# An LSTM step with its gate sums in one scale: reductions for scans, tanh's scale from a register

## The chip, the cores and the metric

One core of one Trainium2 chip. The metric is the device time of one execution in microseconds (us), the median of a few runs. Engines: PE (TensorE), DVE (VectorE), ACT (ScalarE), POOL (GpSimd), SP (SyncE, which starts the DMAs).

## The reference

For x of (2, 1024, 256), an LSTM over 1024 steps with hidden size 256 and batch 2, then a mixture of experts over its 2048 tokens, each added to x:

```
a = xW[t] + h @ Wh                      # xW = x @ Wx + b, (2, 1024) per step
i, f, o = sigmoid(a[:, :256]), sigmoid(a[:, 256:512]), sigmoid(a[:, 512:768])
g = tanh(a[:, 768:])
c = f * c + i * g
h = o * tanh(c)
...
x = x + hs                              # all h
x = x + mixture(x)                      # 2 shared experts, 8 routed ones, top 2, gates by sigmoid
```

## The kernel before

Everything lies in SBUF before it is needed; the 1024 steps are 16 tiles of 64. In each step PE, DVE and ACT do the LSTM (`lstm(s)` on each engine), and behind it each engine takes a slice of the mixture of the tile before (`mixture(s, ...)`, with all slots written out by hand by step number). Tile 0 has `first_tile(s)` in their place; after tile 15 the mixture runs once more without the LSTM. In each of the tiles 1 to 15, PE also makes half of the xW part for the tile after the next one, from fp16 parts of x and Wx (L753): six products after step 0 and six after step 4, and then one after each of the steps 5 to 16.

The product h @ Wh is made of fp16 parts: Wh scaled by a power of two as `wh_hi` + `wh_lo`/4096, h in `hh[..., 0]` (low part) and `hh[..., 1]` (high part, about 4096 h). Each gate column has three neighbouring PSUM columns: one in which `wh_lo` x high part stands (L665), one with `wh_hi` x high part (L672, two columns at once with the low part), and one with the step's xW value (`gif_xw`, `o_xw`), written by DVE from `seeds`, which POOL stages in pieces of 8 steps (`stage`). 8 chunks of 128 gate rows, 4 for g and i (`gi`), 2 for f, 2 for o.

One step of the LSTM, with the lines of the profile:

1. PE: low products of f and gi (L665, 12), high products of f (L672, 4) and gi (8), then low and high of o. `s_mul` counts f, gi, o.
2. DVE: `summed` (L562) forms each gate's sum by a scan, state = factor x state + data, over its three columns; the factors `part_fac` are 0, 1/4096 and the inverse of twice the weight scale. f, then gi, then o.
3. ACT: tanh of the third column: `tf` (L325), g and i into `gi_out` (L328), `to` (L332). sigmoid is made from tanh.
4. DVE: (tanh f + 1) x c (L573), the c scan (L579), seeds of the next step (L585), `to1` = 4096 (to + 1) (L587).
5. ACT: `tc` = tanh of c (L335).
6. DVE: `hh` high part = (to + 1) x tc (L590), `h` = to1 x tc in f32 (L595), `c_now` (L597), o's seed (L601), `hh` low part (L603).

The first weight load of the next step on PE waits for L590 (`s_hhi`), the first high product for L603 (`s_hlo`). DVE works in order; it waits on its own results through `s_own`, which L587 and L595 raise, and on ACT through `s_tanh`.

Of the kernel before, what the change touches and what calls it, by code (L numbers as in the profile page):

```python
# [8 lines left out]
ALU = mybir.AluOpType  # L9
ACT = mybir.ActivationFunctionType  # L10
F32 = mybir.dt.float32
F16 = mybir.dt.float16
U32 = mybir.dt.uint32
AX = mybir.AxisListType
RMAX = bass.bass_isa.ReduceOp.max

P = 128
B, T, D = 2, 1024, 256
KC = D // P
H4 = 4 * D  # L20
MC = H4 // P
HC = KC * B
GATES = MC * B
GI, FG, OG = 4 * B, 2 * B, 2 * B
PARTS = 3
LO = 2.0 ** 12
NTOK = B * T
BANK = 512
TS = 64
TT = TS * B  # L30
NT = T // TS
HS = 8
# [47 lines left out]
def cond_resid_kernel(nc, xT, condT, wx, wh, bT, wr, rb, sw1, sw3, sw2, rw1, rw2, eye, iota, outT):  # L80
    with ExitStack() as ctx:
        def sb(name, shape, dt=F32):
            return ctx.enter_context(nc.sbuf_tensor(name, shape, dt))
# [7 lines left out]
        gates = bank("gates", 3)  # L91
        state, up_sh, up_rt, acc_lg, xw_next = (bank(n) for n in ("state", "up_sh", "up_rt", "acc_lg", "xw_next"))

        gi_ps = gates[:, BANK - PARTS * GI:BANK]
        f_ps = gates[:, BANK:BANK + PARTS * FG]
        o_ps = gates[:, 2 * BANK:2 * BANK + PARTS * OG]
        gif_xw = gates[:, BANK - PARTS * GI:BANK + PARTS * FG].rearrange("p (c j) -> p c j", j=PARTS)[:, :, 2]
        o_xw = o_ps.rearrange("p (c j) -> p c j", j=PARTS)[:, :, 2]

        gi_sum = gates[:, 0:PARTS * GI]  # L100
        f_sum = gates[:, 2 * BANK - PARTS * FG:2 * BANK]
        o_sum = gates[:, 3 * BANK - PARTS * OG:3 * BANK]
        cs = state[:, 0:HC * 3].rearrange("p (c j) -> p c j", j=3)
# [10 lines left out]
        xw = sb("xw", [P, (T + TS) * GATES])  # L114
# [25 lines left out]
        scale = sb("scale", [P, 4, 3])  # L140
        tops, s_wh, s_wx, s_xin = scale[:, 0, :], scale[:, 3, 0:1], scale[:, 3, 1:2], scale[:, 3, 2:3]

        sc = sb("sc", [P, 6])
        unit, one_unit, half_lo, s_wh_lo, wh_g, wh_g_lo = (sc[:, j:j + 1] for j in range(6))
        xw_scale = sb("xw_scale", [P, 2])

        largest = sb("largest", [P, MAX_OF])
        first_banks = (up_sh, up_rt, xw_next, state)
        wh_times_lo = xw[:, TS * GATES:TS * GATES + KC * H4].rearrange("p (k n) -> p k n", k=KC)
        hw0 = sb("hw0", [P, GATES])  # L150
        hh = sb("hh", [P, KC, B, 2], F16)
        h32 = sb("h32", [P, 2, HS, HC])
        seeds = sb("seeds", [P, 2, HS, GATES])

        part_fac = sb("part_fac", [P, GI, PARTS])

# [87 lines left out]
        def _(pool):  # L244
# [10 lines left out]
            def stage(q, first):  # L255

                g.tensor_copy(seeds[:, q % 2, :, :].rearrange("p s g -> p (s g)"), xw[:, first]).then_inc(s_staged, 1)

# [53 lines left out]
        def _(act):  # L312
            activation = nc.scalar.activation
            nc.scalar.preload_act_table(ACT.Gelu)

            act.wait_ge(s_scale, 4)
            for dst, dst_lo, src, by, by_lo in ((wh_hi[:, :, 0:D], wh_times_lo[:, :, 0:D], wh_sb[:, :, 0:D], wh_g, wh_g_lo),
                                                (wh_hi[:, :, D:H4], wh_times_lo[:, :, D:H4], wh_sb[:, :, D:H4], s_wh, s_wh_lo)):
                activation(dst, src, ACT.Identity, scale=by)
                activation(dst_lo, src, ACT.Identity, scale=by_lo).then_inc(s_hi, 1)  # L320

            def lstm(s):

                act.wait_ge(s_sum, 4 * s + F_OF)
                activation(tf[:], f_sum.rearrange("p (c j) -> p c j", j=PARTS)[:, :, PARTS - 1], ACT.Tanh, scale=0.5).then_inc(s_tanh, 1)  # L325

                act.wait_ge(s_sum, 4 * s + GI_OF)
                activation(gi_out, gi_sum.rearrange("p (g c j) -> p g c j", g=2, j=PARTS)[:, :, :, PARTS - 1], ACT.Tanh,  # L328
                           scale=0.5).then_inc(s_scan, 1)

                act.wait_ge(s_sum, 4 * s + O_OF)
                activation(to[:], o_sum.rearrange("p (c j) -> p c j", j=PARTS)[:, :, PARTS - 1], ACT.Tanh, scale=0.5).then_inc(s_tanh, 1)  # L332

                act.wait_ge(s_sum, 4 * s + C_OF)
                activation(tc[:], cs[:, :, 2], ACT.Tanh, scale=0.5).then_inc(s_tanh, 1)  # L335
# [51 lines left out]
        def _(dve):  # L387
# [3 lines left out]
            def link(ins):  # L391

                done[0] += 1
                ins.then_inc(s_link, 1)
                dve.wait_ge(s_link, done[0])
# [10 lines left out]

            link(v.memset(part_fac[:], 1.0))
            link(v.memset(part_fac[:, :, 0], 0.0))
            link(v.memset(part_fac[:, :, 1], 1.0 / LO))
            link(v.memset(fac_add[:], 1.0))  # L410
# [15 lines left out]

            for dst, src, by in ((unit, s_wh, 2.0), (s_wh_lo, s_wh, LO), (wh_g, s_wh, 2.0)):
                v.tensor_scalar(dst, src, by, None, ALU.mult).then_inc(s_scale, 1)
            v.tensor_scalar(wh_g_lo, s_wh, 2.0 * LO, None, ALU.mult).then_inc(s_scale, 1)
            dve.wait_ge(s_scale, 4)  # L430
            link(v.reciprocal(one_unit, unit))
            link(v.tensor_copy(part_fac[:, :, 2], one_unit.broadcast_to([P, GI])))
            dve.wait_ge(s_xw0, 48)
# [9 lines left out]

            for j, (lo, hi, chunks) in enumerate(((0, D, range(0, 4)), (D, H4, range(4, MC)))):
                for m in chunks:
                    first_xw(m)
                dve.wait_ge(s_hi, j + 1)
                v.scalar_tensor_tensor(wh_lo[:, :, lo:hi], wh_hi[:, :, lo:hi], -LO, wh_times_lo[:, :, lo:hi],
                                       ALU.mult, ALU.add).then_inc(s_lo, 1)
            dve.wait_ge(s_xwc0, MC)  # L450
# [4 lines left out]
            dve.wait_ge(s_xwc0, MC + 1)  # L455
            v.tensor_copy(gif_xw, xw[:, 0:GI + FG])

            v.tensor_copy(o_xw, xw[:, GI + FG:GATES]).then_inc(s_hhi, 1)
            v.memset(hw0[:], 0.0).then_inc(s_hlo, 1)
# [99 lines left out]

            def summed(dst, ps, n):  # L560

                return v.tensor_tensor_scan(dst, part_fac[:, 0:n, :].rearrange("p c j -> p (c j)"), ps, 0.0, ALU.mult, ALU.add)  # L562

            def lstm(s):
                piece, at = s // HS, s % HS

                dve.wait_ge(s_mul, 3 * s + F_OF)
                summed(f_sum, f_ps, FG).then_inc(s_sum, 1)
                dve.wait_ge(s_mul, 3 * s + GI_OF)
                summed(gi_sum, gi_ps, GI).then_inc(s_sum, 1)  # L570

                dve.wait_ge(s_tanh, 3 * s + TF_OF)
                v.scalar_tensor_tensor(addend[:, :, 2], tf[:], 1.0, c_now[:], ALU.add, ALU.mult).then_inc(s_scan, 1)  # L573
                dve.wait_ge(s_mul, 3 * s + O_OF)
                summed(o_sum, o_ps, OG).then_inc(s_sum, 1)

# [4 lines left out]
                if at == 0:  # L581
# [7 lines left out]
                dve.wait_ge(s_tanh, 3 * s + TC_OF)  # L589
                v.scalar_tensor_tensor(hh[:, :, :, 1], to[:].rearrange("p (k b) -> p k b", b=B), 1.0,  # L590
                                       tc[:].rearrange("p (k b) -> p k b", b=B), ALU.add, ALU.mult).then_inc(s_hhi, 1)

                h_now = h32[:, piece % 2, at, :]
                dve.wait_ge(s_own, 2 * s + 1)
                v.tensor_tensor(h_now, to1[:], tc[:], ALU.mult).then_inc(s_own, 1)  # L595

                ins = v.tensor_scalar(c_now[:], cs[:, :, 2], 0.5, None, ALU.mult)  # L597
                if at in (STAGE_AT, HS - 1):
# [3 lines left out]
                dve.wait_ge(s_own, 2 * s + 2)  # L602
                v.scalar_tensor_tensor(hh[:, :, :, 0], hh[:, :, :, 1], -LO, h_now.rearrange("p (k b) -> p k b", b=B),  # L603
                                       ALU.mult, ALU.add).then_inc(s_hlo, 1)

# [264 lines left out]
```

## Time and profile before

| | |
|---|---|
| Median of 3 runs | 2158.12 us (2157.96 to 2159.33) |
| Span of the profiled execution | 2157.6 us, 94124 instructions |
| PE | 2037.5 us busy, 94% |
| DVE | 1725.5 us busy, 80%, 13239 instructions |
| ACT | 861.0 us busy, 40% |
| POOL | 136.5 us busy, 6% |
| The three scans of L562, 3072 in all | 591.9 us |

Busy times are of one profiled execution, from its first instruction to its last. Its time without the profiler isn't known apart; the span stands 0.5 us below the median of the runs. The granted clock of PE is 0.5 of full speed from about 24 us to the end of the last LSTM step. Matmuls overlap, so that PE's busy share says little of the room left on it.

### The profile page before, as it was taken

To read this page: it belongs to the slowest core of one execution; us is meant where nothing else is said; L and a number is where in the kernel's file an instruction comes from. 1 tells how busy PE (TensorE), PEld (TensorE's weight loads), DVE (VectorE), ACT (ScalarE), POOL (GpSimd) and SP (SyncE) were. 2 spreads that over 40 slices of the span, in tenths; PEclk is the share of its full clock that TensorE was granted. 3 is DMA by queue.
4 is the path that set the end of the run, shared out by engine and by line. 5 is a ranking of instruction groups with operands and counts; after the bars stand their busy time and mean duration, and the time that the engine had idled before them with its cause. 6 is when DMAs were issued, how large, how long until landed. Compare 5 with 4: busy or idle time off the path is not lost. (4 is left out here: it accounts for less than half of the span.)

```text
span 2157.6 us, 94124 instructions
## 1 busy us (share of the span) xinstructions
PE 2037.5 (94%) x37356; PEld 1862.5 (86%) x37356; DVE 1725.5 (80%) x13239; ACT 861.0 (40%) x4505; POOL 136.5 (6%) x457
## 2 busy tenths in 40 slices
PE   8999989899898989989899898998989999898998
PEld 7889979798897979989799797998979889797998
DVE  7888878788787878878788787887878788787884
ACT  4554334344343434434343333443334344343442
POOL 0000000000000000000000000000000000000000
PEclk7555555555555555555555555555555555555557
DMA  5000000000000000000000000000000000000000
GB/s 218 3 3 3 3 5 3 6 3 2 6 3 6 3 5 3 3 6 3 6 3 3 6 3 6 3 3 6 3 6 3 5 3 2 6 3 6 3 3 6
DMA packets 7218, 20.02 MB, mean 9 GB/s; under 512 B 1136, under 2 KB 5616, under 8 KB 5872
## 3 DMA queue, kind: packets, MB, share of 16 engines
q1 hardware_dynamic: 6768, 13.73, 1.7%
q8 instruction: 318, 5.21, 1.0%
q14 instruction: 132, 1.08, 0.2%
HBM read 11.63 MB, written 2.10 MB: 6 GB/s over the span
## 5 line engine op out<-in xcount | busy, mean ns | idle before, releaser
L562 DVE TENSOR_TENSOR_SCAN gates<-part_fac,gates 128x12 f32<-128x12 f32 (+1 forms) x3072 | 591.9, 193 | 373.8 <-PE gates L672 326.1
L665 PE MATMUL gates<-hh,wh_lo 128*128 128x2 f16 x16384 | 749.4, 168 | 103.7 <-issue 90.9
L665 PEld LDWEIGHTS gates<-hh,wh_lo 128*128 128x128 f16 x16384 | 604.8, 105 | 275.5 <-DVE hh L590 154.4
L672 PE MATMUL gates<-hh,wh_hi 128*128 128x4 f16 x16384 | 690.7, 167 | 3.6 <-DVE hh L603 3.6
L672 PEld LDWEIGHTS gates<-hh,wh_hi 128*128 128x128 f16 x16384 | 595.2, 104 | 5.0 <-DVE hh L603 5.0
L325 ACT ACTIVATE tf<-gates 128x4 f32<-128x4 f32 x1024 | 178.1, 174 | 910.8 <-DVE gates L562 908.5
L679 PE MATMUL up_rt<-xt,rw_sb 128*128 128x128 f32 x1024 | 297.1, 445 | 0.6 <-DVE hid_rt L529 0.5
L685 PE MATMUL acc_lg<-hid_rt,rw_sb 128*128 128x128 f32 x1024 | 296.8, 445 | 0.0
L679 PEld LDWEIGHTS up_rt<-xt,rw_sb 128*128 128x128 f32 x1024 | 230.9, 314 | 1.4 <-DVE hid_rt L529 1.4
L685 PEld LDWEIGHTS acc_lg<-hid_rt,rw_sb 128*128 128x128 f32 x1024 | 230.9, 314 | 0.2 <-DVE hid_rt L529 0.2
L332 ACT ACTIVATE to<-gates 128x4 f32<-128x4 f32 x1024 | 177.7, 174 | 121.4 <-DVE gates L562 42.3
L328 ACT ACTIVATE fac_add<-gates 128x8 f32<-128x8 f32 x1024 | 185.4, 181 | 64.9
L579 DVE TENSOR_TENSOR_SCAN state<-fac_add 128x12 f32<-128x12 f32 x1024 | 195.9, 191 | 0.0
L335 ACT ACTIVATE tc<-state 128x4 f32<-128x4 f32 x1024 | 177.7, 174 | 2.6
L587 DVE TENSOR_SCALAR to<-to 128x4 f32<-128x4 f32 x1024 | 174.6, 170 | 4.2
L573 DVE SCALAR_TENSOR_TENSOR fac_add<-tf,c_now 128x4 f32<-128x4 f32 x1024 | 173.1, 169 | 3.8
L590 DVE SCALAR_TENSOR_TENSOR hh<-to,tc 128x4 f16<-128x4 f32 x1024 | 170.3, 166 | 5.7
L603 DVE SCALAR_TENSOR_TENSOR hh<-hh,h 128x4 f16<-128x4 f16 x1024 | 165.9, 162 | 0.0
L595 DVE TENSOR_TENSOR h<-to,tc 128x4 f32<-128x4 f32 x1024 | 159.5, 156 | 0.0
L597 DVE TENSOR_SCALAR c_now<-state 128x4 f32<-128x4 f32 x1024 | 158.9, 155 | 0.0
L601 DVE COPY gates<-seeds 128x4 f32<-128x4 f32 x1024 | 158.6, 155 | 0.0
L585 DVE COPY gates<-seeds 128x12 f32<-128x12 f32 x1024 | 158.0, 154 | 0.0
(129 smaller groups left out, 1814.6 us busy)
## 6 DMA issues: line engine op xcount, KB each, us to landing
rw_sb<-rw SPq DMA_DIRECT2D x2, 2048.0 KB, 23.1
sw_sb<-sw SPq DMA_DIRECT2D x3, 1024.0 KB, 13.1
outT<-osb SPq DMA_DIRECT2D x16, 128.0 KB, 3.9
x_sb<-xT SPq DMA_DIRECT2D x1, 1920.0 KB, 9.4
wh_sb<-wh SPq DMA_DIRECT2D x1, 1024.0 KB, 4.7
wx_sb<-wx SPq DMA_DIRECT2D x1, 1024.0 KB, 6.9
x_sb<-xT SPq DMA_DIRECT2D x1, 128.0 KB, 5.2
eye_sb<-eye SPq DMA_DIRECT2D x1, 64.0 KB, 5.4
```

The source lines that it names most:

```text
L325: activation(tf[:], f_sum.rearrange("p (c j) -> p c j", j=PARTS)[:, :, PARTS - 1], ACT.Tanh, scale=0.5).then_inc(s_tanh, 1)
L328: activation(gi_out, gi_sum.rearrange("p (g c j) -> p g c j", g=2, j=PARTS)[:, :, :, PARTS - 1], ACT.Tanh, scale=0.5).then_inc(s_scan, 1)
L332: activation(to[:], o_sum.rearrange("p (c j) -> p c j", j=PARTS)[:, :, PARTS - 1], ACT.Tanh, scale=0.5).then_inc(s_tanh, 1)
L335: activation(tc[:], cs[:, :, 2], ACT.Tanh, scale=0.5).then_inc(s_tanh, 1)
L562: return v.tensor_tensor_scan(dst, part_fac[:, 0:n, :].rearrange("p c j -> p (c j)"), ps, 0.0, ALU.mult, ALU.add)
L573: v.scalar_tensor_tensor(addend[:, :, 2], tf[:], 1.0, c_now[:], ALU.add, ALU.mult).then_inc(s_scan, 1)
L579: v.tensor_tensor_scan(cs.rearrange("p c j -> p (c j)"), fac.rearrange("p c j -> p (c j)"), addend.rearrange("p c j -> p (c j)"), 0.0, ALU ...
L587: v.tensor_scalar(to1[:], to[:], 1.0, LO, ALU.add, ALU.mult).then_inc(s_own, 1)
L665: mm(columns(ps, j)[:, :, 0], wh_lo[:, c, (m0 + j) * P:(m0 + j + 1) * P], hh[:, c, :, 1], start=(j == 0 and c == 0), stop=False, skip_grou ...
L672: last = mm(columns(ps, j)[:, :, 0:2], wh_hi[:, c, (m0 + j) * P:(m0 + j + 1) * P], hh[:, c, :, :], start=False, stop=True, skip_group_chec ...
L679: last = mm(ps, w[:, c, at:at + P], xt[:, c, :], start=(c == 0), stop=(c == KC - 1))
L685: ins = mm(acc[:, k * TT:(k + 1) * TT], w[:, k * P:(k + 1) * P], hid, start=(first and k == 0), stop=last, skip_group_check=True)
```

## The change

The xW columns are multiplied by 2 x 4096 x the weight scale (`sums_by`) when they are staged by POOL (for the first step, by DVE), `hh`'s low part is no longer divided by anything, and so all three columns of a gate have one scale. In detail:

- `summed` becomes a reduction over the three columns (`tensor_reduce`, add), with 4 or 8 outputs side by side. `part_fac` goes.
- The three tanh activations of the gates read those, and take their scale (0.5 before) from an ACT register `by_sums`, loaded once in the setup from `to_tanh`. The `tc` activation keeps its 0.5.
- `hh`'s high part is now to1 x tc, with DVE's wait for to1 (`s_own`) in front of it, which stood ahead of L595 before. `hh`'s low part is a subtraction.
- POOL's staging is a multiplication with a broadcast scale in place of a copy.
- In the setup ACT makes only `wh_hi`; `wh_lo` is made by DVE from `wh_sb` straight. Some one-column scales go and others come.

```diff
--- before.py
+++ after.py
@@ -97,9 +97,9 @@
         gif_xw = gates[:, BANK - PARTS * GI:BANK + PARTS * FG].rearrange("p (c j) -> p c j", j=PARTS)[:, :, 2]
         o_xw = o_ps.rearrange("p (c j) -> p c j", j=PARTS)[:, :, 2]
 
-        gi_sum = gates[:, 0:PARTS * GI]
-        f_sum = gates[:, 2 * BANK - PARTS * FG:2 * BANK]
-        o_sum = gates[:, 3 * BANK - PARTS * OG:3 * BANK]
+        gi_sum = gates[:, 0:GI]
+        f_sum = gates[:, 2 * BANK - FG:2 * BANK]
+        o_sum = gates[:, 3 * BANK - OG:3 * BANK]
         cs = state[:, 0:HC * 3].rearrange("p (c j) -> p c j", j=3)
 
         xw_first = [xw_next[:, 0:TT], up_rt[:, 0:TT]]
@@ -140,19 +140,16 @@
         scale = sb("scale", [P, 4, 3])
         tops, s_wh, s_wx, s_xin = scale[:, 0, :], scale[:, 3, 0:1], scale[:, 3, 1:2], scale[:, 3, 2:3]
 
-        sc = sb("sc", [P, 6])
-        unit, one_unit, half_lo, s_wh_lo, wh_g, wh_g_lo = (sc[:, j:j + 1] for j in range(6))
+        sc = sb("sc", [P, 5])
+        sums_by, twice_by, to_tanh, half_lo, wh_g = (sc[:, j:j + 1] for j in range(5))
         xw_scale = sb("xw_scale", [P, 2])
 
         largest = sb("largest", [P, MAX_OF])
         first_banks = (up_sh, up_rt, xw_next, state)
-        wh_times_lo = xw[:, TS * GATES:TS * GATES + KC * H4].rearrange("p (k n) -> p k n", k=KC)
         hw0 = sb("hw0", [P, GATES])
         hh = sb("hh", [P, KC, B, 2], F16)
         h32 = sb("h32", [P, 2, HS, HC])
         seeds = sb("seeds", [P, 2, HS, GATES])
-
-        part_fac = sb("part_fac", [P, GI, PARTS])
 
         fac_add = sb("fac_add", [P, 2, HC, 3])
         fac, addend = fac_add[:, 0, :, :], fac_add[:, 1, :, :]
@@ -254,7 +251,8 @@
 
             def stage(q, first):
 
-                g.tensor_copy(seeds[:, q % 2, :, :].rearrange("p s g -> p (s g)"), xw[:, first]).then_inc(s_staged, 1)
+                g.tensor_tensor(seeds[:, q % 2, :, :].rearrange("p s g -> p (s g)"), xw[:, first],
+                                sums_by.broadcast_to([P, HS * GATES]), ALU.mult).then_inc(s_staged, 1)
 
             stage(0, slice(GATES, (HS + 1) * GATES))
 
@@ -313,23 +311,24 @@
             activation = nc.scalar.activation
             nc.scalar.preload_act_table(ACT.Gelu)
 
-            act.wait_ge(s_scale, 4)
-            for dst, dst_lo, src, by, by_lo in ((wh_hi[:, :, 0:D], wh_times_lo[:, :, 0:D], wh_sb[:, :, 0:D], wh_g, wh_g_lo),
-                                                (wh_hi[:, :, D:H4], wh_times_lo[:, :, D:H4], wh_sb[:, :, D:H4], s_wh, s_wh_lo)):
-                activation(dst, src, ACT.Identity, scale=by)
-                activation(dst_lo, src, ACT.Identity, scale=by_lo).then_inc(s_hi, 1)
+            act.wait_ge(s_scale, 2)
+            for dst, src, by in ((wh_hi[:, :, 0:D], wh_sb[:, :, 0:D], wh_g), (wh_hi[:, :, D:H4], wh_sb[:, :, D:H4], s_wh)):
+                activation(dst, src, ACT.Identity, scale=by).then_inc(s_hi, 1)
+
+            act.wait_ge(s_scale, 3)
+            by_sums = nc.scalar.alloc_register("by_sums")
+            nc.scalar.reg_load(by_sums, to_tanh[0:1, :].bitcast(U32))
 
             def lstm(s):
 
                 act.wait_ge(s_sum, 4 * s + F_OF)
-                activation(tf[:], f_sum.rearrange("p (c j) -> p c j", j=PARTS)[:, :, PARTS - 1], ACT.Tanh, scale=0.5).then_inc(s_tanh, 1)
+                activation(tf[:], f_sum, ACT.Tanh, scale=by_sums).then_inc(s_tanh, 1)
 
                 act.wait_ge(s_sum, 4 * s + GI_OF)
-                activation(gi_out, gi_sum.rearrange("p (g c j) -> p g c j", g=2, j=PARTS)[:, :, :, PARTS - 1], ACT.Tanh,
-                           scale=0.5).then_inc(s_scan, 1)
+                activation(gi_out, gi_sum.rearrange("p (g c) -> p g c", g=2), ACT.Tanh, scale=by_sums).then_inc(s_scan, 1)
 
                 act.wait_ge(s_sum, 4 * s + O_OF)
-                activation(to[:], o_sum.rearrange("p (c j) -> p c j", j=PARTS)[:, :, PARTS - 1], ACT.Tanh, scale=0.5).then_inc(s_tanh, 1)
+                activation(to[:], o_sum, ACT.Tanh, scale=by_sums).then_inc(s_tanh, 1)
 
                 act.wait_ge(s_sum, 4 * s + C_OF)
                 activation(tc[:], cs[:, :, 2], ACT.Tanh, scale=0.5).then_inc(s_tanh, 1)
@@ -404,9 +403,6 @@
                 link(v.tensor_scalar(scale[:, 3, at], scale[:, 2, at], 2.0 ** 13, None, ALU.mult))
 
 
-            link(v.memset(part_fac[:], 1.0))
-            link(v.memset(part_fac[:, :, 0], 0.0))
-            link(v.memset(part_fac[:, :, 1], 1.0 / LO))
             link(v.memset(fac_add[:], 1.0))
             link(v.memset(fac[:, :, 0], 0.0))
             link(v.memset(c_now[:], 0.0))
@@ -424,12 +420,11 @@
             dve.wait_ge(s_top, 1)
             power(slice(0, 1))
 
-            for dst, src, by in ((unit, s_wh, 2.0), (s_wh_lo, s_wh, LO), (wh_g, s_wh, 2.0)):
-                v.tensor_scalar(dst, src, by, None, ALU.mult).then_inc(s_scale, 1)
-            v.tensor_scalar(wh_g_lo, s_wh, 2.0 * LO, None, ALU.mult).then_inc(s_scale, 1)
-            dve.wait_ge(s_scale, 4)
-            link(v.reciprocal(one_unit, unit))
-            link(v.tensor_copy(part_fac[:, :, 2], one_unit.broadcast_to([P, GI])))
+            for dst, by in ((wh_g, 2.0), (twice_by, 4.0 * LO)):
+                v.tensor_scalar(dst, s_wh, by, None, ALU.mult).then_inc(s_scale, 1)
+            link(v.tensor_scalar(sums_by, s_wh, 2.0 * LO, None, ALU.mult))
+            dve.wait_ge(s_scale, 2)
+            v.reciprocal(to_tanh, twice_by).then_inc(s_scale, 1)
             dve.wait_ge(s_xw0, 48)
             link(v.tensor_scalar(b_twice[:], b_sb[:, 0:KC], 2.0, None, ALU.mult))
 
@@ -441,21 +436,21 @@
                                 b_sb[:, m:m + 1], 2.0 if m < KC else 1.0, ALU.add, ALU.mult).then_inc(s_xwc0, 1)
 
 
-            for j, (lo, hi, chunks) in enumerate(((0, D, range(0, 4)), (D, H4, range(4, MC)))):
+            for j, (lo, hi, by, chunks) in enumerate(((0, D, wh_g, range(0, 4)), (D, H4, s_wh, range(4, MC)))):
                 for m in chunks:
                     first_xw(m)
                 dve.wait_ge(s_hi, j + 1)
-                v.scalar_tensor_tensor(wh_lo[:, :, lo:hi], wh_hi[:, :, lo:hi], -LO, wh_times_lo[:, :, lo:hi],
-                                       ALU.mult, ALU.add).then_inc(s_lo, 1)
+                v.scalar_tensor_tensor(wh_lo[:, :, lo:hi], wh_sb[:, :, lo:hi], by, wh_hi[:, :, lo:hi],
+                                       ALU.mult, ALU.subtract).then_inc(s_lo, 1)
             dve.wait_ge(s_xwc0, MC)
             v.tensor_tensor(xw[:, 0:GATES], xw[:, 0:GATES], hw0[:], ALU.add).then_inc(s_xwc0, 1)
 
             take_back(dve, s_lg, 1)
             link(v.tensor_copy(tpart[:], logits))
             dve.wait_ge(s_xwc0, MC + 1)
-            v.tensor_copy(gif_xw, xw[:, 0:GI + FG])
-
-            v.tensor_copy(o_xw, xw[:, GI + FG:GATES]).then_inc(s_hhi, 1)
+            v.tensor_scalar(gif_xw, xw[:, 0:GI + FG], sums_by, None, ALU.mult)
+
+            v.tensor_scalar(o_xw, xw[:, GI + FG:GATES], sums_by, None, ALU.mult).then_inc(s_hhi, 1)
             v.memset(hw0[:], 0.0).then_inc(s_hlo, 1)
 
             lg, nl, e, num, dn, sg, mask, t0, t1, t2 = (rt[:, j, :] for j in range(10))
@@ -557,22 +552,22 @@
                     take_back(dve, s_free, 1)
                     v.tensor_tensor(osb[:], acc.rearrange("p (k t) -> p k t", k=KC), xt[:], ALU.add).then_inc(s_fin, 1)
 
-            def summed(dst, ps, n):
-
-                return v.tensor_tensor_scan(dst, part_fac[:, 0:n, :].rearrange("p c j -> p (c j)"), ps, 0.0, ALU.mult, ALU.add)
+            def summed(dst, ps):
+
+                return v.tensor_reduce(dst, ps.rearrange("p (c j) -> p c j", j=PARTS), AX.X, ALU.add)
 
             def lstm(s):
                 piece, at = s // HS, s % HS
 
                 dve.wait_ge(s_mul, 3 * s + F_OF)
-                summed(f_sum, f_ps, FG).then_inc(s_sum, 1)
+                summed(f_sum, f_ps).then_inc(s_sum, 1)
                 dve.wait_ge(s_mul, 3 * s + GI_OF)
-                summed(gi_sum, gi_ps, GI).then_inc(s_sum, 1)
+                summed(gi_sum, gi_ps).then_inc(s_sum, 1)
 
                 dve.wait_ge(s_tanh, 3 * s + TF_OF)
                 v.scalar_tensor_tensor(addend[:, :, 2], tf[:], 1.0, c_now[:], ALU.add, ALU.mult).then_inc(s_scan, 1)
                 dve.wait_ge(s_mul, 3 * s + O_OF)
-                summed(o_sum, o_ps, OG).then_inc(s_sum, 1)
+                summed(o_sum, o_ps).then_inc(s_sum, 1)
 
                 dve.wait_ge(s_scan, 2 * s + 2)
 
@@ -587,11 +582,11 @@
                 v.tensor_scalar(to1[:], to[:], 1.0, LO, ALU.add, ALU.mult).then_inc(s_own, 1)
 
                 dve.wait_ge(s_tanh, 3 * s + TC_OF)
-                v.scalar_tensor_tensor(hh[:, :, :, 1], to[:].rearrange("p (k b) -> p k b", b=B), 1.0,
-                                       tc[:].rearrange("p (k b) -> p k b", b=B), ALU.add, ALU.mult).then_inc(s_hhi, 1)
+                dve.wait_ge(s_own, 2 * s + 1)
+                v.tensor_tensor(hh[:, :, :, 1], to1[:].rearrange("p (k b) -> p k b", b=B),
+                                tc[:].rearrange("p (k b) -> p k b", b=B), ALU.mult).then_inc(s_hhi, 1)
 
                 h_now = h32[:, piece % 2, at, :]
-                dve.wait_ge(s_own, 2 * s + 1)
                 v.tensor_tensor(h_now, to1[:], tc[:], ALU.mult).then_inc(s_own, 1)
 
                 ins = v.tensor_scalar(c_now[:], cs[:, :, 2], 0.5, None, ALU.mult)
@@ -600,8 +595,8 @@
 
                 v.tensor_copy(o_xw, seeds[:, piece % 2, at, GI + FG:GATES])
                 dve.wait_ge(s_own, 2 * s + 2)
-                v.scalar_tensor_tensor(hh[:, :, :, 0], hh[:, :, :, 1], -LO, h_now.rearrange("p (k b) -> p k b", b=B),
-                                       ALU.mult, ALU.add).then_inc(s_hlo, 1)
+                v.tensor_tensor(hh[:, :, :, 0], h_now.rearrange("p (k b) -> p k b", b=B), hh[:, :, :, 1],
+                                ALU.subtract).then_inc(s_hlo, 1)
 
             def round_end():
                 take_back(dve, s_mul, 3 * TS)
```

## Rows read from the trace of the kernel before

**Rows 1.** Waits: engine, tile and line waited for; us in total, times, longest us

```profile
PEld gates L665 <- DVE hh L590: 154.4, 829, 1.7
PEld gates L665 <- issue: 93.2, 28, 4.4
```

**Rows 2.** Timeline of one step: start us, us, engine, line, work, idle before

```profile
1001.70 0.42 DVE L562 TENSOR_TENSOR_SCAN gates<-part_fac,gates 128x12 f32<-128x12 f32 x2 [0.40 <-PE gates L672]
...
1001.92 0.17 ACT L325 ACTIVATE tf<-gates 128x4 f32<-128x4 f32 x1 [1.10 <-DVE gates L562]
...
1002.13 0.17 DVE L573 SCALAR_TENSOR_TENSOR fac_add<-tf,c_now 128x4 f32<-128x4 f32 x1
1002.16 0.18 ACT L328 ACTIVATE fac_add<-gates 128x8 f32<-128x8 f32 x1
1002.21 0.18 DVE L562 TENSOR_TENSOR_SCAN gates<-part_fac,gates 128x12 f32<-128x12 f32 x1
1002.37 0.19 DVE L579 TENSOR_TENSOR_SCAN state<-fac_add 128x12 f32<-128x12 f32 x1
1002.42 0.17 ACT L332 ACTIVATE to<-gates 128x4 f32<-128x4 f32 x1
...
1002.60 0.17 ACT L335 ACTIVATE tc<-state 128x4 f32<-128x4 f32 x1
1002.63 0.17 DVE L587 TENSOR_SCALAR to<-to 128x4 f32<-128x4 f32 x1
1002.80 0.17 DVE L590 SCALAR_TENSOR_TENSOR hh<-to,tc 128x4 f16<-128x4 f32 x1
...
1003.02 0.40 PEld L665 LDWEIGHTS gates<-hh,wh_lo 128*128 128x128 f16 x12 [0.17 <-DVE hh L590]
```

**Rows 3.** DVE groups by shape: count, busy us, mean ns, idle before

```profile
L562 DVE TENSOR_TENSOR_SCAN gates<-part_fac,gates 128x12 f32<-128x12 f32 x2048 | 375.5, 183 | 347.7 <-PE gates L672 326.1
L562 DVE TENSOR_TENSOR_SCAN gates<-part_fac,gates 128x24 f32<-128x24 f32 x1024 | 217.5, 212 | 26.1
...
L595 DVE TENSOR_TENSOR h<-to,tc 128x4 f32<-128x4 f32 x1024 | 159.5, 156 | 0.0
...
L619 DVE TENSOR_REDUCE largest<-x_sb 128x1 f32<-128x256 f32 x16 | 6.6, 411 | 0.0
...
L475 DVE TENSOR_TENSOR rt<-acc_lg,tpart 128x8 f32<-128x8 f32 x16 | 2.7, 167 | 2.4 <-DVEq L220 2.4
...
L547 DVE TENSOR_REDUCE den<-rt 128x1 f32<-128x8 f32 x16 | 2.4, 153 | 0.0
```

**Rows 4.** Line L522: engine, instruction, count, ns min, median, max, first and last start

```profile
L522 DVEq EVENT_SEMAPHORE  x128: 21/21/21, 159.5 to 2134.4; - x128
```

**Rows 5.** Timeline of DVE in the tail of the span: start us, us, engine, line, work

```profile
2130.47 0.15 DVE L547 TENSOR_REDUCE den<-rt 128x1 f32<-128x8 f32 x1
2130.66 0.15 DVE L504 TENSOR_SCALAR den<-den 128x1 f32<-128x1 f32 x1
...
2132.67 0.29 DVE L517 SCALAR_TENSOR_TENSOR uu<-th,up_sh 128x128 f32<-128x128 f32 x1 [0.39 <-ACT th L359]
2133.06 0.29 DVE L524 SCALAR_TENSOR_TENSOR hid_sh<-uu,up_rt 128x128 f32<-128x128 f32 x1
```

**Rows 6.** Lines L342 and L363 on ACT; ns min, median, max

```profile
L363 ACT ACTIVATE xw<-xw_next,b_sb,xw_scale x60: 458/458/463, 151.3 to 2026.8; 128x128 f32 x60
L342 ACT ACTIVATE xw<-xw_next,b_sb x17: 368/368/373, 27.4 to 146.8; 128x128 f32<-128x128 f32 x17
```

**Rows 7.** Timeline of PE, two of the steps that follow a step with one wx product

```profile
167.19 0.51 PE L665 MATMUL gates<-hh,wh_lo 128*128 128x2 f16 x12
...
169.19 0.51 PE L665 MATMUL gates<-hh,wh_lo 128*128 128x2 f16 x12
```

**Rows 8.** Timeline of POOL, one staging copy

```profile
1001.33 0.29 POOL L257 COPY seeds<-xw 128x128 f32 x1 [13.09 <-DVE c_now L597]
```

**Rows 9.** Group of the costliest POOL multiply

```profile
L263 POOL TENSOR_TENSOR x_scaled<-x_sb,scale 128x256 f32<-128x256 f32 x16 | 9.8, 614 | 0.0
```

## The prediction

> **What bounds the kernel now.** I read the totals first, then the list of waits, then the timeline of one step, and last the groups by shape for durations. PE is busy 94% of the span, but the waits say that it is not the bound: in 829 of the 1024 steps the first weight load of a step (L665) stands idle until DVE has written hh at L590 [rows 1]. In another 180 steps (12 in each of 15 tiles, the ones in which one fp16 product for the next tile's wx part stands last on PE) the load is let in at the same moment, but the array is still streaming. In the 15 first steps of a tile PE is late by itself, part of the 28 waits put down to "issue" [rows 1]. So the time is 1024 turns of one loop of dependent work, some 1.95 us each, and what counts is the distance round it.
>
> In the timeline of a step [rows 2] count from the f scan at 1001.70. The f scan and its hand-over bring ACT to tf at +0.22; tf and a hand-over bring DVE to L573 at +0.43; the o scan follows at +0.51; ACT takes `to` at +0.72; L587 (to1) runs from +0.93 to +1.10. This is the **output branch**. The **cell branch** starts with the gi scan at +0.21, goes through L328 (+0.46), the c scan L579 (+0.67) and `tc` (+0.90), and ends at +1.07. L590 starts at +1.10, 0.03 after the end of `tc`, and this is where the reader should look: to1 ends at the very moment at which L590 starts. Today L590 doesn't read to1. After the change it does. Each hand-over from one engine to another costs 0.03 to 0.04 us.
>
> **The sums.** The three scans become reductions with as many columns in and a third as many out. A scan of 12 columns takes 183 ns and one of 24 takes 212 [rows 3]. No multi-output reduction is in the trace; the nearest are 8 columns to one in 153 ns and 256 to one in 411, a slope of 258/248 = 1.04 ns a column [rows 3]. That gives 157 ns for 12 columns and 170 for 24. They read PSUM; an addition of 8 columns with one PSUM operand takes 167 against 156 for 4 columns from SBUF [rows 3], of which 4 are columns, so I add 8: **165 and 178**. The f and o reductions then take 18 ns less each, gi 34 less. Below, the bound is no PSUM surcharge (26 less each); above, a reduction that pays for each of its outputs and so costs what the scan does (0 less). I take 18, since the rows it rests on are of the same instruction.
>
> The output branch holds two of these terms (f, o): to1 ends 0.036 earlier, at +1.064. The cell branch holds only gi, since the gi scan is let in by PE and not by the f scan's end: `tc` ends 0.034 earlier, at +1.036.
>
> The Trainium skill ("VectorE: DVE Perf Modes", Rules for kernel authors) calls `tensor_reduce` the slowest DVE operation on a hot path and advises against it. The rows have it at 153 ns where the 12-column scan takes 183 [rows 3]; by the page nothing would be saved, and the sum below would be 2158 + 829 x 0.095 + 180 x 0.045 = 2245 us.
>
> **The hi part of h (L590), the term that decides.** It becomes a product of to1 and tc, with two waits in front: tc's and, second, DVE's own for to1. No arithmetic instruction of this trace holds two waits. Where the program asks for two, as ahead of L524, the second becomes an instruction of its own, L522, 21 ns on the queue, 128 times [rows 4]. It costs little when it was satisfied long before. What it costs when it is satisfied last can be read in the last tile's mixture [rows 5]: L517 ends at 2132.67 + 0.29 = 2132.96, L522 waits for it, and L524 starts at 2133.06, that is **0.10 us** after the end. A single wait on DVE's own result, L504 behind L547, is over in 0.04 (2130.47 + 0.15 to 2130.66) [rows 5]. The new L590 has exactly L524's form, and its second wait is the one satisfied last (to1 at +1.064 against `tc` at +1.036). So it starts at 1.064 + 0.10 = +1.164, where it was +1.10: 0.064 later. A product is a little shorter than the two-operation form: 156 ns for L595 [rows 3] against 0.17 for L590 [rows 2]; L590 starts from an idle engine, so I take 5 ns off, 10 at most. In sum: **hh is ready 0.06 us later in a step**, and PE, which was waiting for it, starts 0.06 later.
>
> Behind L590 on DVE stand h (L595), c_now, the o seed and the lo part; all start some 0.06 later together. The lo part is wanted by PE's high products only after twelve low ones, which move too, so nothing is added. L595 loses its own wait, which was satisfied anyway.
>
> **How many steps pay.** 829 pay 0.06: 49.7 us. In the 180 steps with the wx product, the first products of two successive ones start at 167.19 and 169.19, 2.00 us apart [rows 7], against 1.95 elsewhere: 0.05 is lost because PE is still busy when hh comes. A later hh uses that up, so these pay 0.06 - 0.05 = 0.01: 1.8 us. The 15 first steps pay nothing. Sum 51.5 us.
>
> **tanh's scale from a register.** ACT's three activations keep shape and operands. The only rows with a register on ACT are L363's, whose output address is in one: it takes 458 ns where L342 takes 368 [rows 6], but it also has a scale pointer more. A register that is only read, with no arithmetic on it, has no row. Bounds: 0 below; above, the whole 90 ns on each of tf, gi and `to`. I take 0, because an address in a register and a second pointer together cost no more than 90, and the new scale is neither a pointer nor computed; the upper end is a rival.
>
> **Edits at nothing.** POOL's staging becomes a multiply. The copy takes 0.29 us from 1001.33 [rows 8]; a multiply of twice the columns takes 614 ns [rows 9], so at most 0.61. Its result is wanted by the seed copy behind the c scan of the step after the one shown [rows 2], at 1002.37 + 1.95 = 1004.3, so 2.4 us of cover remain; without it each 0.3 us would cost 128 x 0.3 = 38 us. The setup loses two long ACT passes and three small memsets and gains pointer scales: all before 33 us of 2158, mostly under loads and first products, +/- 0.5 us. The lo part's form (subtract in place of multiply-add) is off the loop.
>
> The profiled span is 2157.6 us and the median 2158.1, 0.5 apart for launch and end; I add the sum to the median: 2158.1 + 51.5 = **2210 us**.
>
> **The rivals.**
> *A (0.71), the forecast.* Its own range, 2190 to 2250: shortest reductions (0.052 less) and 10 ns off L590 give +0.038 a step, 829 x 0.038 = 32 us, 2190; reductions as dear as scans and no shorter product give +0.10, 829 x 0.10 + 180 x 0.05 = 92 us, 2250.
> *B (0.08), faster: the second wait costs what a single one does.* Then hh starts at the later of 1.064 + 0.035 and 1.036 + 0.03, at +1.10 as before, and only the shorter product is left, 5 to 10 ns; 829 x 0.007 = 6 us less, **2152**. With the shortest reductions it is 0.023 a step, 2139. It decides if the time from to1's end to L590 is under 0.036 + 0.007 = 0.043 us. For it: the wait is satisfied just about when tc's is. Against it: the 0.10 of L524 [rows 5]. The Trainium skill ("VectorE: DVE Perf Modes", The DRAIN you can't avoid) says that semaphores between DVE operations cost nothing extra, which is this case; its measurement chained one wait each, and the row of L524 shows 0.10 with two [rows 5].
> *C (0.09): the register costs 90 ns at each activation.* The output branch holds tf and `to`: +0.18 a step on top, 829 x 0.24 + 180 x 0.19 = 233 us, **2391**. For it: the 90 ns between L363 and L342 [rows 6]; against it: the second pointer, which explains them.
> *D (0.09): the separate wait is tc's and to1's rides on L590.* Then hh starts at 1.036 + 0.10 = +1.136, 0.036 late, 0.03 after the shorter product: 829 x 0.03 = 25 us, **2183**. Against it: at L522 it is the second one that stands alone.
> The last 0.03 is for what no row shows.
>
> **Numbers.** A and D, 0.80, lie between 2180 and 2250, which is the range. Under 0.2% (4.3 us) the measurement can't tell a change from none. Faster: B and a little, 0.09. Same: 0.03. Slower: 0.88.
>
> **What would show it.** A new separate wait in each step between L587 and the product, 21 ns, starting some 0.04 after to1's end; hh starting 0.10 after to1's end and not 0.03 after tc's; reductions of about 165 and 178 ns; a step of 2.01 us in place of 1.95, but 2.01 for 2.00 in the wx steps; ACT's durations at 0.17 and 0.18 us as before. It is wrong if hh follows `tc` by 0.03, if tf and `to` are longer or start later behind their sums than 0.03, or if a reduction takes over 200 ns.

## The result, and the profile after

The changed kernel takes 2261.9 us (median of 4 runs, 2260.8 to 2262.1) against 2158.7 of the kernel before on the same chip: a ratio of 1.047 (1.046 to 1.049), 103 us slower. Forecast were 2210 us and a range of 2180 to 2250. The direction and the main mechanism (the wait that is split off) hold. The size is twice the one forecast, and over half of what is missing lies in places that the sum had at nothing.

The waits of the kernel after, to be read against [rows 1]:

```profile
PEld gates L660 <- DVE hh L586: 284.1, 1009, 9.4
PEld gates L660 <- issue: 92.8, 28, 4.6
...
POOL seeds L254 <- issue: 18.2, 1, 18.2
...
DVE gates L580 <- POOL seeds L254: 8.8, 1, 8.8
```

PE now waits for the high part of h in every step but the first of each of 15 tiles (1009 times in place of 829), and 130 us longer in all. The last two rows are new, and no part of the prediction.

One step on DVE and ACT, to be read against [rows 2]:

```profile
1053.56 0.41 DVE L557 TENSOR_REDUCE gates<-gates 128x4 f32<-128x12 f32 x2 [0.41 <-PE gates L667]
1053.98 0.17 DVE L568 SCALAR_TENSOR_TENSOR fac_add<-tf,c_now 128x4 f32<-128x4 f32 x1
1054.06 0.17 DVE L557 TENSOR_REDUCE gates<-gates 128x4 f32<-128x12 f32 x1
1054.21 0.19 DVE L574 TENSOR_TENSOR_SCAN state<-fac_add 128x12 f32<-128x12 f32 x1
1054.31 0.15 DVE L580 COPY gates<-seeds 128x12 f32<-128x12 f32 x1
1054.47 0.17 DVE L582 TENSOR_SCALAR to<-to 128x4 f32<-128x4 f32 x1
1054.75 0.17 DVE L586 TENSOR_TENSOR hh<-to,tc 128x4 f16<-128x4 f32 x1
```

```profile
1053.78 0.17 ACT L325 ACTIVATE tf<-gates 128x4 f32<-128x4 f32 x1 [1.20 <-DVE gates L557]
1054.00 0.18 ACT L328 ACTIVATE fac_add<-gates 128x8 f32<-128x8 f32 x1
1054.27 0.17 ACT L331 ACTIVATE to<-gates 128x4 f32<-128x4 f32 x1
1054.44 0.17 ACT L334 ACTIVATE tc<-state 128x4 f32<-128x4 f32 x1
```

`tc` ends at 1054.61 and to1 (L582) at 1054.64, both earlier in the step than before (+1.05 and +1.08 from the f reduction, before +1.07 and +1.10). L586 starts at 1054.75: 0.11 behind to1, 0.14 behind `tc`, where L590 started 0.03 behind `tc`. Between them stands a wait of its own, one for each step:

```profile
L585 DVEq EVENT_SEMAPHORE  x1024: 21/21/21, 31.5 to 2221.4; - x171
```

It starts 0.038 us behind to1's end, takes 0.021, and L586 starts 0.045 behind it: 0.104 in all, as the median of the 1024 steps. The step, taken as the median distance of two f reductions, went from 1.953 to 2.033 us.

The groups by shape, against [rows 3]:

```profile
L557 DVE TENSOR_REDUCE gates<-gates 128x4 f32<-128x12 f32 x2048 | 359.0, 175 | 335.7 <-PE gates L667 313.5
L557 DVE TENSOR_REDUCE gates<-gates 128x8 f32<-128x24 f32 x1024 | 196.4, 192 | 34.8
...
L586 DVE TENSOR_TENSOR hh<-to,tc 128x4 f16<-128x4 f32 x1024 | 170.0, 166 | 117.7 <-DVE to L582 14.2
L590 DVE TENSOR_TENSOR h<-to,tc 128x4 f32<-128x4 f32 x1024 | 167.9, 164 | 3.7 <-issue 3.7
...
L596 DVE COPY gates<-seeds 128x4 f32<-128x4 f32 x1024 | 159.2, 155 | 2.5 <-issue 2.5
```

The reductions take 175 and 192 ns (forecast 165 and 178). L586 is no shorter than L590 was. And DVE is idle for "issue" ahead of L590 and L596, which no row of before shows. Where that is can be seen in two steps of the ninth tile, first its step 27 and then its step 10:

```profile
1183.47 0.17 DVE L582 TENSOR_SCALAR to<-to 128x4 f32<-128x4 f32 x1
1184.10 0.17 DVE L586 TENSOR_TENSOR hh<-to,tc 128x4 f16<-128x4 f32 x1 [0.46 <-DVE to L582]
```

```profile
1148.69 0.17 DVE L586 TENSOR_TENSOR hh<-to,tc 128x4 f16<-128x4 f32 x1
1149.09 0.16 DVE L590 TENSOR_TENSOR h<-to,tc 128x4 f32<-128x4 f32 x1 [0.22 <-issue]
```

Steps 10, 18, 27 and 56 of each tile after the first take 2.31, 2.24, 2.39 and 2.39 us for 2.03, and step 48 takes 2.71 (2.50 before, when a step was 0.08 shorter). In all these tiles the same instruction of the program comes late: L586 in step 27, L590 in step 10. The page's row for the queue that brings instructions in had 132 packets before and has 15 more, one for each pass through the tile loop:

```profile
q14 instruction: 147, 1.20, 0.2%
```

The last new thing is in the first step, on POOL:

```profile
12.25 0.38 POOL L247 PARTITION_ALL_REDUCE wtop<-wmax  x1 [10.10 <-issue]
30.80 0.39 POOL L254 TENSOR_TENSOR seeds<-xw,sc 128x128 f32<-128x128 f32 x1 [18.17 <-issue]
```

POOL's wait for the first xW ends at 20.5 us, and the first staging runs at 30.8. In between stand two configuration instructions of POOL, at 20.7, and then nothing for 10 us:

```profile
L254 POOLq MODIFY_POOL_CONFIG  x4: 11/46/83, 20.7 to 102.3; - x4
```

DVE's seed copy (L580) waits 8.8 us for this staging.

**The 102.3 us between the two spans (2157.6 and 2259.9)** are made up so: the step, 829 x 0.080 = 66.3; the 180 steps with a wx product, 2.000 before and 2.033 now, 180 x 0.033 = 5.9; the stalls at fixed steps, some 1.34 a tile (1.2 in steps 10, 18, 27 and 56, the rest in 46 and 48), 15 x 1.34 = 20; the first step 8.8. That makes 101.

### The profile page after: what moved, and what is told of

It reads as the page before. It is cut to its first block and busy times, and to the rows that moved or that the text cites. A ratio compares the mean times of both kernels' runs of the same rounds, so it can differ in the third digit from the quotient of the medians.

```text
span 2259.9 us, 95142 instructions
## 1 busy us (share of the span) xinstructions
PE 2111.0 (93%) x37356; PEld 1854.6 (82%) x37356; DVE 1690.0 (75%) x13234; ACT 858.6 (38%) x4503; POOL 150.0 (7%) x457
## 5 line engine op out<-in xcount | busy, mean ns | idle before, releaser
L660 PEld LDWEIGHTS gates<-hh,wh_lo 128*128 128x128 f16 x16384 | 595.2, 105 | 379.4 <-DVE hh L586 284.1
L557 DVE TENSOR_REDUCE gates<-gates 128x4 f32<-128x12 f32 (+1 forms) x3072 | 554.9, 181 | 370.5 <-PE gates L667 313.5
L586 DVE TENSOR_TENSOR hh<-to,tc 128x4 f16<-128x4 f32 x1024 | 170.0, 166 | 117.7 <-DVE to L582 14.2
L582 DVE TENSOR_SCALAR to<-to 128x4 f32<-128x4 f32 x1024 | 174.7, 171 | 7.2
L254 POOL TENSOR_TENSOR seeds<-xw,sc 128x128 f32<-128x128 f32 x129 | 51.8, 401 | 1832.1 <-DVE c_now L592 1813.9
L590 DVE TENSOR_TENSOR h<-to,tc 128x4 f32<-128x4 f32 x1024 | 167.9, 164 | 3.7 <-issue 3.7
L580 DVE COPY gates<-seeds 128x12 f32<-128x12 f32 x1024 | 158.4, 155 | 8.8 <-POOL seeds L254 8.8
L596 DVE COPY gates<-seeds 128x4 f32<-128x4 f32 x1024 | 159.2, 155 | 2.5 <-issue 2.5
L598 DVE TENSOR_TENSOR hh<-h,hh 128x4 f16<-128x4 f32 x1024 | 159.9, 156 | 0.0
```

Of the source, the lines that this page charges most:

```text
L557: return v.tensor_reduce(dst, ps.rearrange("p (c j) -> p c j", j=PARTS), AX.X, ALU.add)
L582: v.tensor_scalar(to1[:], to[:], 1.0, LO, ALU.add, ALU.mult).then_inc(s_own, 1)
L660: mm(columns(ps, j)[:, :, 0], wh_lo[:, c, (m0 + j) * P:(m0 + j + 1) * P], hh[:, c, :, 1], start=(j == 0 and c == 0), stop=False, skip_grou ...
```

## The experiments

Each ran against the kernel before on the same chip, which took 2157 us beside experiments 1 to 4, 2161 beside 5, 6, 7 and 9, and 2160 beside 8. The kernel after (2261.9) ran beside a kernel before of 2158.7, so a difference of an experiment from the kernel after holds to about 2 us.

**1. The order of the two waits** (`e1_waits_swapped`), the kernel after with

```diff
-                dve.wait_ge(s_tanh, 3 * s + TC_OF)
                 dve.wait_ge(s_own, 2 * s + 1)
+                dve.wait_ge(s_tanh, 3 * s + TC_OF)
```

> The kernel after, with the two waits ahead of the high part of h (L586) in the other order, so that the wait that stands alone is the one for tc and the one for to1 rides on L586. Theory 1 (a wait that stands alone costs 0.104 us from the end of what it waits for to the instruction behind it, a riding one 0.035): L586 starts 0.104 behind the end of tc, at 1.155 us from the f reduction in place of 1.186, and the step falls from 2.033 to 2.002 us; 1009 steps by 0.031 are 31 us, so 2231 us. The extra stalls at four or five fixed steps of each tile stay, since DVE's queue still stands at a wait. Rival 2 (the 0.104 is the price of reading to1 so soon after DVE wrote it, whichever way one waits): the order changes nothing, 2262 us.

Measured: 2226.2 us (ratio 1.032, 1.030 to 1.033), step 2.000 us. L586 moved with the end of the thing for which the lone wait stands. Its timeline on ACT, and on DVE:

```profile
1055.01 0.17 ACT L334 ACTIVATE tc<-state 128x4 f32<-128x4 f32 x1
```

```profile
1055.05 0.17 DVE L582 TENSOR_SCALAR to<-to 128x4 f32<-128x4 f32 x1
1055.29 0.17 DVE L586 TENSOR_TENSOR hh<-to,tc 128x4 f16<-128x4 f32 x1
```

`tc` ends at 1055.18 and L586 starts 0.11 later (0.10 as the median of all steps); behind to1's end, 1055.22, it is now only 0.07. So reading to1 early is not what costs: of two waits the one written second stands alone on the queue, and what it waits for is paid with 0.10. It is paid even here, where that wait is satisfied 0.03 ahead of the other. Rival 2 is out.

**2. The old high part** (`e2_old_high_part`), the kernel after with

```diff
-LO = 2.0 ** 12
+LO = 1.0
...
                 dve.wait_ge(s_tanh, 3 * s + TC_OF)
-                dve.wait_ge(s_own, 2 * s + 1)
-                v.tensor_tensor(hh[:, :, :, 1], to1..., tc..., ALU.mult).then_inc(s_hhi, 1)
+                v.scalar_tensor_tensor(hh[:, :, :, 1], to..., 1.0, tc..., ALU.add, ALU.mult).then_inc(s_hhi, 1)
                 h_now = h32[:, piece % 2, at, :]
+                dve.wait_ge(s_own, 2 * s + 1)
```

> The kernel after, with the high part of h made as before from to and tc by one instruction that waits for tc alone, and the wait for to1 back ahead of L590. The factor 4096 on h is set to 1 so that all parts keep one scale. Theory 1: L586 starts 0.033 behind tc, at 1.084 in place of 1.186; the step falls to 1.931 us, and to 2.00 in the 180 steps in which PE is busy longer: 829 x 0.102 + 180 x 0.03 = 90 us; if the extra stalls inside a tile (some 1.3 us in each of 15) come from the queue that stands at the wait, they go too, 20 us: 2152 us. If they come from the number or kind of DVE instructions they stay: 2172 us. Rival 2 (reductions or the register cost the time): under 20 us less, over 2240 us.

Measured: 2153.1 us (ratio 0.998, 0.997 to 0.999): the whole loss is gone with this one line and its wait, from 103 us over the kernel before to 4 us under it, and what stays of the change is a small gain. POOL's late first staging is still in it: the first step takes 11.6 us. The step is 1.933 us, the queue for instructions is back at 132 packets, and no step of a tile is long but the one that was before. Its timeline:

```profile
1051.05 0.41 DVE L557 TENSOR_REDUCE gates<-gates 128x4 f32<-128x12 f32 x2 [0.41 <-PE gates L667]
...
1051.96 0.17 DVE L582 TENSOR_SCALAR to<-to 128x4 f32<-128x4 f32 x1
1052.14 0.17 DVE L585 SCALAR_TENSOR_TENSOR hh<-to,tc 128x4 f16<-128x4 f32 x1
```

L585 (the high part, here) is at +1.09 where it was at +1.10 before and at +1.19 after.

**3. The scans back** (`e3_scans_back`), the kernel after with `tensor_tensor_scan` in `summed`, factors 0, 1, 1, and tanh reading each third column.

> The kernel after, with the scans in place of the reductions (all factors 1, the first of each gate column 0), tanh reading each third column as before. Theory 1: the f scan takes 188 ns for 179, gi 213 for 192, o 180 for 172; f and o lie ahead of to1, so L586 starts 0.017 later and the step takes 2.050 us: 1009 x 0.017 = 17 us more, 2279 us. The rule of the Trainium skill (VectorE: DVE Perf Modes, Rules for kernel authors) that tensor_reduce is the slowest operation on a hot path would make this kernel faster than the one after, under 2262 us.

Measured: 2269.0 us (ratio 1.052, 1.050 to 1.053), 7 to 9 us over the kernel after, not 17. The step is 0.014 longer, 2.047 us, near the 0.017 expected (14 us in all). Part of that is given back by the stalls: here only steps 18 (2.32), 46 (2.47) and 48 (2.70) are long. The groups by shape:

```profile
L561 DVE TENSOR_TENSOR_SCAN gates<-part_fac,gates 128x12 f32<-128x12 f32 x2048 | 374.1, 183 | 341.7 <-PE gates L671 317.9
L561 DVE TENSOR_TENSOR_SCAN gates<-part_fac,gates 128x24 f32<-128x24 f32 x1024 | 216.7, 212 | 27.6
```

So a reduction saves 8 to 9 ns of 183 and 20 of 212. The rule of the Trainium skill (VectorE: DVE Perf Modes, Rules for kernel authors) that `tensor_reduce` is the slowest on a hot path doesn't hold against this scan.

**4. POOL switched early** (`e4_pool_switched_early`), the kernel after with

```diff
             g.partition_all_reduce(wtop[:, 0:1], wmax[:, 0:1], P, RMAX).then_inc(s_top, 1)
+            g.memset(warm[:, 0:4], 0.0).then_inc(s_warm, 1)
+            pool.wait_ge(s_warm, 1)
+            g.tensor_tensor(warm[:, 4:8], warm[:, 0:4], warm[:, 0:4], ALU.mult).then_inc(s_warm, 1)
```

> The kernel after, with a multiplication of 4 columns by POOL right behind its first reduction over partitions, ahead of the wait for the first xW. Theory 1: the 10 us between POOL's configuration instructions and its first multiplication (L254) are spent while the setup runs on the other engines, from 12.3 to about 22.4 us, when the first staging would begin; the first step, 10.8 us now, takes about 2.0 to 3: 8 to 9 us less, 2253 us. Rival: the configuration is loaded again for L254, or the wait of 10 us has another cause (the xW data): 2262 us.

Measured: 2254.2 us (ratio 1.045, 1.043 to 1.046), 6 to 8 us less; the first step takes 2.3 us in place of 10.8. POOL's timeline:

```profile
11.98 0.38 POOL L249 PARTITION_ALL_REDUCE wtop<-wmax  x1 [9.84 <-issue]
12.23 0.17 POOL L250 MEMSET warm<- 128x4 f32 x1
22.36 0.19 POOL L252 TENSOR_TENSOR warm<-warm 128x4 f32<-128x4 f32 x1 [9.96 <-issue]
22.52 0.39 POOL L259 TENSOR_TENSOR seeds<-xw,sc 128x128 f32<-128x128 f32 x1
```

The 10 us stand between the configuration instructions and the first multiplication behind the reduction over partitions, and they moved with that multiplication. The kernel before has such a gap too (7 us, from 35.5 to 42.5 us, ahead of its first L278, and again 7 us, from 99.6 to 106.9, behind its second reduction). But its first staging is a copy, which ran 0.2 us behind its wait, and DVE was not held up by the late multiplication. What POOL does in these microseconds no row shows.

**5. The register alone** (`e5_before_register`), the kernel before with its three 0.5 from a register.

> The kernel before, with the 0.5 of the three gate activations read from an ACT register that is loaded once in the setup. Theory 1: the register costs nothing, tf, gi and to keep 0.174, 0.181 and 0.174 us and start 0.034 behind their sums: 2157 to 2159 us. Rival C of the prediction (90 ns at each): over 2300 us.

Measured: 2160.3 us against 2160.7 (ratio 1.000, 0.999 to 1.001). Durations of tf, gi and `to` and their distances from the sums are the same to the nanosecond or two. Rival C of the prediction is out.

**6. The new high part alone** (`e6_before_new_high_part`), the kernel before with

```diff
-LO = 2.0 ** 12
+LO = 1.0
...
                 dve.wait_ge(s_tanh, 3 * s + TC_OF)
-                v.scalar_tensor_tensor(hh[:, :, :, 1], to..., 1.0, tc..., ALU.add, ALU.mult).then_inc(s_hhi, 1)
+                dve.wait_ge(s_own, 2 * s + 1)
+                v.tensor_tensor(hh[:, :, :, 1], to1..., tc..., ALU.mult).then_inc(s_hhi, 1)
                 h_now = h32[:, piece % 2, at, :]
-                dve.wait_ge(s_own, 2 * s + 1)
```

> The kernel before, with the high part of h made from to1 and tc as in the kernel after, behind the two waits; the factor 4096 on h is set to 1 so that all parts keep the scales that the scan's factors take out. Theory 1: L590's instruction starts 0.104 behind to1's end, at 1.202 us in place of 1.104, the step goes from 1.953 to 2.051: 829 x 0.098 + 180 x 0.051 = 90 us; with some 20 us of new stalls inside the tiles, if these come from DVE's queue that stands at the wait, 2268 us; 2248 if they come from anything else in the change. Rival 2 (it takes the reductions or the staging to lose the time): under 2180 us.

Measured: 2263.1 us (ratio 1.047, 1.046 to 1.049): this line of the change alone costs as much as the whole change. That the two agree so closely is partly chance: the whole change has POOL's 9 us and more stalls on top, and the reductions' gain against them. The step is 2.047 us, and steps 1, 36, 46 and 48 of a tile take 2.14, 2.23, 2.40 and 2.71.

**7. A wait that is never waited for** (`e7_before_spare_wait`), the kernel before with

```diff
                 dve.wait_ge(s_tanh, 3 * s + TC_OF)
+                if s:
+                    dve.wait_ge(s_own, 2 * s)
```

> The kernel before, with a second wait ahead of L590, for the h of the step before, which is long there: DVE gets the same 64 waits a tile more as the kernel after, but none at which its queue stands. Theory 1 (what costs is the release, 0.104 behind the last thing waited for, and the stalls inside a tile come from a queue held at a wait): L590 stays 0.033 behind tc and no step is over 2.2 us but those that were: 2157 to 2162 us. Rival 3 (the stalls come from the number of DVE instructions): the step stays at 1.953 us but four or five steps of each tile take 0.2 to 0.35 longer, 15 x 1.3 = 20 us: 2178 us. Rival 4 (a wait that stands alone costs its 21 + 45 ns even when it is satisfied): 2158 + 829 x 0.066 = 2213 us.

Measured: 2166.8 us against 2160.7 (ratio 1.003, 1.002 to 1.004). The lone wait is there 1008 times (L591), the high part (L592) still starts 0.03 behind `tc`, and the step is 1.954 us; rival 4 is out. But the time is 6 us up, and two steps of each tile are long, 18 (2.21) and 46 (2.10). Step 18 in its timeline:

```profile
1111.58 0.17 DVE L587 TENSOR_SCALAR to<-to 128x4 f32<-128x4 f32 x1
1112.02 0.17 DVE L592 SCALAR_TENSOR_TENSOR hh<-to,tc 128x4 f16<-128x4 f32 x1 [0.26 <-DVE to L587]
```

The instruction queue has its 147 packets here too. So neither theory is whole: stalls do come without a queue that stands at the new wait, 0.4 us a tile, but not the 1.34 of the kernel after.

**8. The other way round** (`e9_count_of_before`), the kernel after without L596, so that DVE has as many instructions as before and its queue still stands at the wait. It leaves the output gate's xW out of the sums, so it computes something else, and only its time counts.

> The kernel after without L596: o's xW of the steps from 1 on is left out of the sums, and DVE has as many instructions per step as in the kernel before, while its queue still stands at the wait for to1 (L585). The step stays 2.033 us, since L596 is off the loop. Theory 5 (a queue held at a wait can't run ahead to the next block of instructions, and the stalls of 0.2 to 0.35 us at fixed steps of a tile are what this lays bare; the 64 instructions more only shift and add to them): there are still stalls at steps that have none in the kernel before, about 1 us in each tile, and the time is 2255 to 2262 us. Rival 3 (the number of instructions alone): they are gone, 15 x 1.4 = 21 us less, 2241 us.

Measured: 2254.4 us (ratio 1.044, 1.042 to 1.046), 7 to 8 us under the kernel after, just under theory 5's range and far from rival 3's 2241. The instruction queue has its 132 packets again, as in the kernel before, and the step is 2.033. Yet steps 6, 15 and 24 take 2.19, 2.30 and 2.21, and 48 still 2.70, where the kernel before has no stall but that at 48. Step 15:

```profile
1154.37 0.17 DVE L586 TENSOR_TENSOR hh<-to,tc 128x4 f16<-128x4 f32 x1
1154.76 0.16 DVE L590 TENSOR_TENSOR h<-to,tc 128x4 f32<-128x4 f32 x1 [0.22 <-issue]
```

So with the queue held at the wait there are stalls, some 0.7 us a tile (0.16 + 0.27 + 0.18, and the 0.12 by which step 48 grew beyond the step's own 0.08), though DVE has no instruction more than before; more instructions add and shift some.

The trace says more of where the stalls stand. Count DVE's instructions, those of its queue with them, from a tile's first f sum: in the kernel after the late ones are number 159 (L590, step 10), 287, 415 (L586, step 27), 671 and 799, in experiment 8 number 95, 223 and 351 (steps 6, 15 and 24), in experiment 7 number 283 and 667. Within a kernel these are 128, or a multiple of it, apart. Each is followed by a packet of 8 KB on the instruction queue, 0.67 us later as the median (0.64 to 0.97). Behind L590 at 1149.09 in step 10 it starts at 1149.76; of the microsecond from 1149 to 1150 the view of the queues has

```profile
q14 instruction: 1, 0.01, 2.8%
```

So the stalls stand at the edges of blocks of 128 instructions, 8 KB. Step 48 is not on this grid; it is long in all kernels. What the late instruction lacks at such an edge stays argued, since the packet that is seen starts only behind it. Nor do the runs part the held queue from the place of the edges in a step. Experiments 6 and 7 come nearest, with the edges one instruction apart: held 0.62 us a tile, not held 0.40, both without step 48.

**9. What is good in the change, without what costs** (`e8_short_output_branch`), the kernel after with experiment 2's and experiment 4's edits and to1 dropped (the counts of `s_own` follow):

```diff
-                dve.wait_ge(s_tanh, 3 * s + TO_OF)
-                v.tensor_scalar(to1[:], to[:], 1.0, LO, ALU.add, ALU.mult).then_inc(s_own, 1)
...
-                v.tensor_tensor(h_now, to1[:], tc[:], ALU.mult).then_inc(s_own, 1)
+                v.scalar_tensor_tensor(h_now, to[:], 1.0, tc[:], ALU.add, ALU.mult).then_inc(s_own, 1)
```

> The kernel after, with the old form of the high part (factor 4096 set to 1), h made from to and tc by the same form, to1 dropped, and POOL switched early. Theory 1: the step is the 1.933 us of the kernel with the old high part (the cell branch sets it), 4 to 5 us less than the kernel before over the 829 steps times 4: 829 x 0.020 = 17 us, tiles the same in the 180 steps, and no 9 us in the first step: 2157 - 17 + 3 = 2143 to 2145 us. Dropping to1 gives nothing of its own. Rival: DVE's room sets the step and each instruction dropped gives its 0.08 us back: under 2100 us.

Measured: 2144.4 us against 2160.7 (ratio 0.993, 0.991 to 0.994), faster than the kernels before and after. The step is 1.933 us as in experiment 2, though DVE has one instruction of 0.17 us less in each. Its waits and timeline show why the drop of to1 gives nothing more:

```profile
DVE hh L587 <- ACT tc L339: 180.5, 1023, 0.2
```

```profile
1051.90 0.19 DVE L579 TENSOR_TENSOR_SCAN state<-fac_add 128x12 f32<-128x12 f32 x1
1052.00 0.15 DVE L585 COPY gates<-seeds 128x12 f32<-128x12 f32 x1
1052.33 0.17 DVE L587 SCALAR_TENSOR_TENSOR hh<-to,tc 128x4 f16<-128x4 f32 x1 [0.18 <-ACT tc L339]
```

DVE now stands idle 0.18 us in each step in to1's place, and the cell branch alone (c scan, `tc`, hand-over) lets L587 go.

## Why the prediction was right in its mechanism and wrong in its size

- **What bounds the kernel: right.** Each step hangs on the distance from the f sum to the high part of h; where that grew, the step grew by as much (by the medians 1.104 to 1.186 us, and 1.953 to 2.033).
- **The split wait: right.** 0.104 us from to1's end to L586, read off one place in the tail at 0.10. Experiments 1, 2 and 6 show it from three sides. B (the wait costs what a single one does) is out, and D's order is that of experiment 1, not the one built.
- **The sums: the term that was mis-sized.** The prediction took 165 and 178 ns from reductions to one output; they took 175 and 192. The f and o terms together gave back 17 ns, not 36. (The 8 ns for reading PSUM are 7 by their own rows, 167 - 156 - 4; that hardly matters.) L586 didn't get shorter (166 ns as before; 5 ns taken). Together this is the 0.08 in place of 0.06: 829 x 0.02 = 17 us, and with it 0.033 for 0.01 in the 180 steps, 4 us.
- **"Edits at nothing": wrong for POOL's staging.** The prediction weighed the multiply's length and cover in the steady state, 2.4 us, and not its first use, and gave the setup +/- 0.5 us. The staging is now the first multiplication behind a reduction over partitions, and DVE waited 8.8 us for it. The trace of before had the sign: 7 us ahead of its first L278, where nothing waited for it.
- **Left out: the stalls.** 20 us. The sum had the split wait at its own 0.10 and nothing for a queue that is held at it, nor for 64 instructions more in a tile. "So nothing is added" behind L590 was wrong: in step 10 it is L590, the h behind the high part, that comes late.
- **C (register): rightly small.** Nothing, by experiment 5. **A's range** held the per-step part (0.038 to 0.10, measured 0.080: 2230 us by it); it had no room for the two terms that stand outside the step. Together the misses, 17 + 4 + 9 + 20 = 50 us, are all but 2 of the 52 us between 2210 and 2262.

## What to carry to other kernels

A second wait ahead of an instruction was an instruction of its own in all these kernels, and it should be the one that is satisfied first, and well ahead: satisfied last it costs 0.10 us where a single one costs 0.03, satisfied 0.03 us before the other it still set the time (experiment 1), and satisfied a step before it cost the step nothing (experiment 7). In a loop of dependent steps such a distance is paid in every step. Make an operand that sits on a shorter branch only where the branch stays shorter by that much; better, read its source again, as the old form did with `to`. When an edit puts a new kind of operation on an engine, look at its first use and at what is queued behind it, not only at its price in the steady state.

## What was not expected of the hardware

- Kernels whose DVE queue stands at a lone wait in each step had 0.7 to 1.3 us of stalls in each tile of 135 to 138 us (experiments 1, 3, 4, 6 and 8, and the kernel after); one with the wait always satisfied had 0.4 us (experiment 7). The late instructions stand 128, or a multiple of it, apart, each with an 8 KB packet of the instruction queue some 0.67 us behind it.
- POOL's first elementwise multiplication after a reduction over partitions came 7 us (kernel before) to 11 us (experiment 2) behind its configuration instructions; a plain copy and a memset in that place didn't wait (kernel before, experiment 4).
- A reduction of three neighbouring PSUM columns to one took 175 ns for 4 outputs and 192 for 8, scans over the same columns 183 and 212.
- A scale from an ACT register cost nothing (2160.3 against 2160.7 us).
